# Routing logits of the attention stage in column groups of the array, turned back by one transpose

## What is computed

```python
x = x + 0.5 * ffn(layernorm(x), router_w, expert_bias, shared_w..., routed_w...)
x = x + attention(layernorm(x), W_q, W_k, W_v, W_o)
x = x + 0.5 * ffn(layernorm(x), router_w, expert_bias, shared_w..., routed_w...)
# in ffn:
scores = sigmoid(x @ router_w)                 # router_w is 256 x 16
_, top_idx = top_k(scores + expert_bias, 2)
```

## Time and profile before

| | us |
|---|---|
| median of 3 runs | 1482.68 |
| the three runs | 1480.43, 1482.68, 1484.01 |
| the profiled execution, its own time | 1479.03 |
| its span | 1477.0 |
| PE busy in the span | 1414.3 (96%) |
| granted TensorE clock, mean | 0.983 of full |

### The profile page before, as it was taken

How to read it: one execution, slowest core, us unless ns; L and a number is a source line. 1 busy time by engine, 2 the same in 40 slices (tenths; PEclk the granted TensorE clock), 3 DMA queues, 4 the chain that set the end, 5 groups by cost and what they waited for, 6 DMA issues and landing times. The chain is left out here.

```text
span 1477.0 us, 28613 instructions
## 1 busy us (share of the span) xinstructions
PE 1414.3 (96%) x8679; PEld 1154.1 (78%) x8712; DVE 956.1 (65%) x2269; ACT 660.6 (45%) x1347; POOL 585.7 (40%) x832
## 2 busy tenths in 40 slices
PE   5999999999989989999999999889999999999998
PEld 2688888888878876667767776568888888888887
DVE  5679865556555667777677766446776456565566
ACT  4534454343433444665666666544322343433332
POOL 6528820233333124464466444401388333333100
PEclk9999999999999998999999999889999999999999
DMA  9997998534396846454655555454464634356941
GB/s 343 332 340 266 329 368 343 183 111 140 104 329 213 300 123 155 96 137 129 148 128 135 142 136 127 156 189 172 150 243 150 231 105 147 104 209 206 306 134 53
DMA packets 175480, 284.75 MB, mean 193 GB/s; under 512 B 20708, under 2 KB 124644, under 8 KB 175092
## 3 DMA queue, kind: packets, MB, share of 16 engines
q1 hardware_dynamic: 133588, 205.26, 43.9%
q0 software_dynamic: 19104, 56.64, 10.6%
q10 hardware_dynamic: 22656, 21.11, 4.8%
HBM read 143.16 MB, written 109.84 MB: 171 GB/s over the span
## 5 line engine op out<-in xcount | busy, mean ns | idle before, releaser
L1717 PE MATMUL f_bank<-f_xparts,f_sw 128*128 128x512 f32 x1536 | 375.1, 394 | 3.4 <-DVEq L1647 3.3
L1717 PEld LDWEIGHTS f_bank<-f_xparts,f_sw 128*128 128x128 f32 x1536 | 282.6, 190 | 58.4 <-DVEq L1647 4.3
L1159 POOL DMA_INDIRECT outputs_by_choice<-f_yr,f_home x160 | 153.7, 960 | 355.4 <-DVE f_yr L1671 293.7
L2332 ACT ACTIVATE at_pT<-at_ps 128x512 f32<-128x512 f32 (+1 forms) x352 | 188.2, 560 | 64.5 <-PE at_ps L2598 58.0
L2260 POOL TENSOR_SCALAR_AFFINE_SELECT at_pT<-at_pT 128x128 f32<-128x128 f32 (+2 forms) x352 | 121.9, 354 | 199.9 <-ACT at_pT L2332 197.6
L1117 POOL DMA_INDIRECT rows_by_slot<-f_xq,slot x128 | 146.6, 1145 | 123.6 <-DVEq L1396 85.3
L1280 ACT CAST f_hparts<-f_hid 128x512 fp32r<-128x512 f32 x128 | 79.4, 620 | 206.8 <-DVE f_hid L1551 206.7
L1660 DVE TENSOR_TENSOR f_sil<-f_sil,f_bank 128x256 f32<-128x256 f32 x160 | 67.5, 422 | 159.9 <-ACT f_sil L1300 156.0
L1551 DVE TENSOR_TENSOR f_hid<-f_sil,f_bank 128x512 f32<-128x512 f32 x128 | 87.7, 685 | 117.7 <-PE f_bank L1717 106.7
L1731 PE MATMUL f_bank<-f_sw,f_hparts 128*128 128x256 f32 x1024 | 146.3, 286 | 2.0 <-ACT f_hparts L1280 1.7
L1731 PEld LDWEIGHTS f_bank<-f_sw,f_hparts 128*128 128x128 f32 x1024 | 137.4, 190 | 12.8 <-ACT f_hparts L1280 4.9
(11 more groups left out here) (268 smaller groups left out, 2665.3 us busy)
## 6 DMA issues: line engine op xcount, KB each, us to landing
f_ring<-weights_in_parts SPq DMA_DIRECT2D x32, 768.0 KB, 5.2
weights_in_parts<-fa_whi SPq DMA_DIRECT2D x30, 768.0 KB, 7.9
f_rawx<-rows_by_slot ACTq DMA_DIRECT2D x152, 128.0 KB, 2.1
at_whi<-weights_in_parts SPq DMA_DIRECT2D x16, 768.0 KB, 8.4
fa_ew<-in_L_ffn_routed_w_dram SPq DMA_DIRECT2D x42, 256.0 KB, 5.0
rows_by_slot<-zero POOLq DMA_DIRECT2D x10, 1024.0 KB, 22.5
f_xq<-xn_rows POOLq DMA_DIRECT2D x32, 256.0 KB, 4.0
fa_ew<-outputs_by_choice SPq DMA_DIRECT2D x8, 1024.0 KB, 8.6
```

Source lines behind the costliest of these rows:

```text
L1159: nc.gpsimd.indirect_dma_start(dram.yk, bass.IndirectOffsetOnAxis(ap=home[:, i:i + 1], axis=0), yr[:, i % 4, :], None).then_inc(y_st[i % 4 ...
L1717: ins = pe.matmul(ps[j % 2][:, :], sw12[:, wp, k, w, j * P:(j + 1) * P], xparts[:, u, xp, k, :], start=(i == 0), stop=(i == 3 * KD - 1))
L2332: s_.activation(pT[:, i % SLOTS, 0:w], ps2[i % RING2][:, 0:w], ACT.Exp).then_inc(ex_done, 1)
```

## The change

`route` now holds the router's 16 columns stationary and moves 128 columns of `xnT2` past them. The four row tiles t go to four column groups: the output of tile t, 16 logits x 128 rows, is on partitions 32t to 32t+15. This is again 8 matmuls. ACT copies the bank, 128 x 128, to a new tile `lT` (`logit_rows`). PE transposes `lT` in one instruction into the next `psX` bank (`spread`), and DVE copies the same 64 numbers per partition to `g.logits`, now out of four pieces 32 apart.

`route` moves from s = 9 to s = 8, directly behind `weigh`. `logit_rows` stands at s = 8 on ACT behind `copy_o`. `spread` and the DVE copy stand at s = 10. `AUX` has one entry more per chunk. The tile `lT` takes 512 bytes per partition of space that was free.

```diff
@@ attention_rows
+    r.lT = m.sb("lT", [P, P])
@@ attention: where the work stands
     def route_of(i, s):
-        return ours(i // NG - 2, 0, NB_) if i % NG == 1 and s == 9 else None
+        return ours(i // NG - 2, 0, NB_) if i % NG == 1 and s == AT_WEIGH else None
+
+    def spread_of(i, s):
+        return ours(i // NG - 2, 0, NB_) if i % NG == 1 and s == AT_WEIGH + 2 else None
@@ ACT, called behind copy_o
+            def logit_rows(c):
+
+                act.wait_ge(*full("route", c))
+                if c >= 1:
+                    act.wait_ge(*full("spread", c - 1))
+                sem, _ = gone("route", c)
+                s_.copy(lT[:], bank("route", c)[:, 0:P]).then_inc(sem, 1)
@@ DVE, called at s = 10 behind maxima
             def logits(c):
 
-                dve.wait_ge(*full("route", c))
-                sem, _ = gone("route", c)
-                v.tensor_copy(g.logits[:, bass.ds(c * (CT * E), CT * E)], bank("route", c)[:, 0:CT * E]
-                              ).then_inc(sem, 1)
+                dve.wait_ge(*full("spread", c))
+                sem, _ = gone("spread", c)
+                v.tensor_copy(g.logits[:, bass.ds(c * (CT * E), CT * E)].rearrange("p (t e) -> p t e", e=E),
+                              bank("spread", c)[:, 0:P].rearrange("p (t e) -> p t e", t=CT)[:, :, 0:E]).then_inc(sem, 1)
@@ PE, route called behind weigh, spread at s = 10 behind score2
-                for t in range(CT):
-                    for k in range(KD):
-                        ins = pe.matmul(bank("route", c)[:, t * E:(t + 1) * E], xnT2[:, k, t * P:(t + 1) * P],
-                                        g.rw[:, k, :], start=(k == 0), stop=(k == KD - 1))
+                for k in range(KD):
+                    for t in range(CT):
+                        ins = pe.matmul(bank("route", c)[32 * t:32 * t + E, 0:P], g.rw[:, k, :],
+                                        xnT2[:, k, t * P:(t + 1) * P], start=(k == 0), stop=(k == KD - 1),
+                                        skip_group_check=True)
                 ins.then_inc(sem, 1)
+
+            def spread(c):
+
+                sem = into("spread", c)
+                pe.wait_ge(*gone("route", c))
+                pe.transpose(bank("spread", c)[:, 0:P], lT[:], g.ident[:, :]).then_inc(sem, 1)
```

More of the change, by code:

```diff
@@ L497, in attention_rows @@
     r.mT = m.sb("mT", [P, 2, P], F32R)
+    r.lT = m.sb("lT", [P, P])
     r.pT = m.sb("pT", [P, len(UNITS1) + 4, CHUNK])
-    used = 4096 + 1024 + 2 * 128 + 512 + 1024 + 512 + 3 * 1024 + 80 + 5 * 1024 + 64 + 448 + 2 * 256 + 15 * CHUNK
+    used = 4096 + 1024 + 2 * 128 + 512 + 1024 + 512 + 3 * 1024 + 80 + 5 * 1024 + 64 + 448 + 2 * 256 + 128 + 15 * CHUNK
     m.sb("rest", [P, n - used])
@@ L2019, in attention @@
         for s in range(UN):
-            for kind, of in (("max", max_of), ("route", route_of), ("proj", proj_of), ("out", out_of),
-                             ("turn2", turn2_of), ("turn", turn_of), ("value", value_of)):
+            for kind, of in (("max", max_of), ("spread", spread_of), ("proj", proj_of), ("out", out_of),
+                             ("turn2", turn2_of), ("route", route_of), ("turn", turn_of), ("value", value_of)):
                 if of(i, s) is not None:
@@ L2035, in attention @@
         sums, turned, rec, attnT = mine.sums, mine.turned, mine.rec, mine.attnT
+        lT = mine.lT
         xres, xn2, xnT2, raw0 = mine.xres, mine.xn2, mine.xnT2, mine.raw0
@@ L2404, in _ @@
                         copy_o(i - 1)
+                    if route_of(i, s) is not None:
+                        logit_rows(route_of(i, s))
                     if turn_of(i, s) is not None:
@@ L2533, in _ @@
                         moments1(c + 2, s - 3)
-                    if route_of(i, s) is not None:
-                        logits(c - 2)
+                    if spread_of(i, s) is not None:
+                        logits(spread_of(i, s))
                     if s == AT_PROJ + 1 and proj_of(i, AT_PROJ) is not None:
@@ L2709, in _ @@
                         score2(u // UN, u % UN)
-                    if route_of(i, s) is not None:
-                        route(route_of(i, s))
+                    if spread_of(i, s) is not None:
+                        spread(spread_of(i, s))
                     if proj_of(i, s) is not None:
@@ L2719, in _ @@
                         weigh(i - 1)
+                    if route_of(i, s) is not None:
+                        route(route_of(i, s))
                     if turn_of(i, s) is not None:
```

## The result

| | before | after |
|---|---|---|
| median of 7 runs each, us | 1481.43 | 1472.86 |
| lowest and highest | 1478.37, 1484.01 | 1469.78, 1476.43 |
| the profiled execution | 1479.03 | 1471.12 |
| its span | 1477.0 | 1469.1 |

The ratio is 0.9945, with a 95% interval of 0.993 to 0.996: the change takes 8.6 us (0.55%) off. The forecast was 7.25 us less, 1475.4 us, with a range of 1472.0 to 1480.0. In a second comparison the same two kernels stood at 1475.56 and 1482.26 us, ratio 0.9948 (0.993 to 0.997), 6.7 us.

A forecast was written before the change was run, and what follows sets the result against it. PE was taken to bound the kernel, with DVE late just behind it at project_out. Six chunks' 6.0 us plus 1.25 us of clock, off the 1482.68 us median, gave 1475.4 us, range 1472 to 1480.

The forecast's parts named there:

- The bound: Attention stage: PE busy 226.91 of 230 us, so time leaving PE leaves the kernel unless another engine is late behind it.
- Removed, 1.71 us: PE, chunks 0 to 5: the old route's 16 records, 1.71 us from its start to the next score, go.
- The route, 0.46 us: PE behind weigh: the new route moves 512 columns at 0.89 ns each with four groups at once, 0.46 us a chunk.
- from above: Upper estimate for the new route on PE: groups in turn, 16 records of 0.114 us each, 1.83 us.
- The transpose, 0.1: PE, one added transpose per chunk: between zero and 0.15 us, taken as 0.1.
- DVE's chain: Maxima, logits copy and scale ahead of project_out: replayed, project_out starts 0.94 us earlier; gain taken as 1.0 a chunk, 6.0 for six.
- ACT's copy, nothing: ACT behind copy_o: the added 128 x 128 copy takes at most 0.39 us and costs nothing, with 0.45 us of cover.
- Chunk 6, nothing: Block's end: no gain or loss; the new chain ends near 973.0, 0.9 us inside the store's cover.
- The clock, 1.25 us: PE behind chunk 4's route: the clock's fall goes with the old route, 1.25 us back; other executions none or two.
- It comes back as a wait: Rival: late transposed logits or a longer DVE chain lose half of the 6.0 and the clock's part; 1479.7 us, chance 0.10.
- One group after another: Rival: column groups run in turn, +0.22 us on PE, DVE's chain later, +2.6 for six; 1485.3 us, chance 0.06.
- The loads are not hidden: Rival: each record also costs its load, route up to 3.6 us, some 2.2 us a chunk slower; 1496 us, chance 0.04.

The follow-up runs named there:

- after_four: Changed kernel with the 8 matmuls of each route issued four times; 64 records hold PE 1.86 us, ratio to the kernel before 0.9997.
- one_group: Changed kernel with all four row tiles in one column group, four transposes instead of one; route 1.84 us, ratio to the kernel before 0.9993.
- dve_three: Changed kernel with DVE copying the transposed logits three times; weigh's last record to the next round's 14.14 us, against 13.88 in the changed kernel.
- act_three: Changed kernel with ACT copying the route's bank three times; weigh's last record to the next round's 13.88 us, as in the changed kernel.
- tile_outer: Changed kernel with route's two loops exchanged, each row tile's matmuls together; route 0.57 us, ratio to the kernel before 0.9948.
- no_route: Changed kernel without the route, its copy, the transpose and the logits of chunks 0 to 6; median 1474.38 us against 1475.56, ratio to the kernel before 0.9941.
- after_again: Changed kernel, unchanged, for a second trace and comparison; median 1475.56 us, ratio to the kernel before 0.9948.

## Why the prediction was right

*The bound.* PE was the bound of the stage, and time taken from it left the kernel: the stretch, the round and the kernel fell together. But at project_out it was DVE, before and after, as the replay said. What no part of the prediction named are the DMAs of `at_rec` and `fa_qT` behind DVE; in chunk 0 they took 0.4 to 0.5 us of the gain in each of the two traces.

*Removed, 1.71 us:* as it was.

*The route, 0.46 us:* from weigh's last record to the score of s = 9 it was 0.20 us before and is 0.64 now, so 0.44. `after_four` gives the same 0.44, and `one_group` shows what it would be without the groups, 1.84 (1.83 given for "from above").

*The transpose, 0.1:* 0.03 us to its neighbour. It slips in under the scores around it; the lower bound was the right one.

*DVE's chain:* foreseen 0.94 us of gain, taken 1.0, measured 1.12 (project_out itself stands 1.10 us nearer to weigh). The steps were right and a little large: the copy costs 0.13 and not 0.2 (`dve_three`), and one maxima follows the other after 0.61 us and not 0.65. PE would have gained 1.71 - 0.44 - 0.03 = 1.24. So the term was mis-sized by 0.12 us a chunk: 6.7 us for six, not 6.0, less the 0.4 of chunk 0.

*ACT's copy, nothing:* right (`act_three`). It took 0.27 us, under the bound of 0.39.

*Chunk 6, nothing:* right. These are the lines that answer to the earlier trace rows; the last two are the copy of its logits on DVE and the next block's first matmul; the fence behind is the store's time to landing:

```profile
962.46 0.58 SPq L2235 DMA_DIRECT2D xn_turned<-at_xnT  x1
962.53 0.63 PE L2712 MATMUL at_psX<-at_xnT,rw 128*16 128x128 f32 x16 [1.61 <-ACT at_xnT L2387]
...
963.62 0.45 PE L2721 MATMUL at_psX<-ident,at_lT 128*128 128x128 f32 x1 [0.47 <-ACT at_lT L2395]
964.11 0.22 DVE L2514 COPY logits<-at_psX 128x64 f32<-128x64 f32 x1 [0.79 <-PE at_psX L2721]
...
966.55 0.77 PE L1718 MATMUL f_bank<-f_xparts,f_sw 128*128 128x512 f32 x1 [2.48 <-DVEq L1648]
```

```profile
xn_turned<-at_xnT SPq DMA_DIRECT2D x1, 512.0 KB, 3.1
```

The logits are there at 964.33, and the store, 3.1 us behind its issue, lands near 965.6. Before, the next block began 4.09 us behind the issue of the store (970.80 and 974.89), and now too (962.46 and 966.55).

*The clock, 1.25 us:* two traces of the kernel before show one fall behind a route each, at different chunks; with doubled routes there were three. In ten traces of kernels whose route moves 128 columns per load, 60 routes, there is none. That the fall came with the old route and went with it is supported by these counts, though the clock also fell where no route was near (926.0 in the kernel before). What of the route it was is not settled: the kind of matmul, its length and its place changed together, `after_four` and `one_group` match the length but stand behind weigh, and six routes each without a fall are weak evidence against one in six. The prediction stopped at chunk 4, and over the whole block the clock gave back nothing: in the two rounds behind chunk 5's it was 0.77 in both traces of the kernel before and 0.66 and 0.64 in those of the changed one, and they took 1.2 and 1.9 us longer. Of the other kernels made from the changed one, `tile_outer` has 0.77 and 22.03 us, the rest 0.64 to 0.71 and 22.83 to 23.85 us; `no_route`, with no route at all, is among them (0.70, 23.09 us). Whether the change lowers the clock there, or chance does, is open.

*The number, and luck.* The forecast was 7.25 us less, and the medians fell by 8.6 and 6.7 us. The six rounds, which are what the prediction was about, fell by 7.5 in both pairs. That the whole agrees with it is in part luck: 1.2 to 1.9 us were lost at the block's end, which the prediction did not foresee, and the time ahead of the first route and in the rounds without one varies by more than that.

*The rivals.* "It comes back as a wait" did not happen: project_out waited for DVE before and does now. Its wait grew from 0.11 to 0.24 us, which is the 0.12 us that DVE did not pass on; it was 0.69 in the one chunk of `after_again` where the DMA was late. "One group after another" is `one_group`, and the groups do work at once. "The loads are not hidden": 16 loads of 0.097 us, 1.55 us together, lie in a stream of 0.44 us. The 16 loads of `one_group`, as long, lie in 1.84 us of records that follow each other without a gap, so they overlap within one column group too. By the rule of the Trainium skill (TensorE: Matmul & The Clock Gate, The mechanism) a load overlaps matmuls in flight only in another row group; all groups here use all rows, and the loads overlap. The trace disagrees with that rule, and decides; a sentence of the same section that also lets a load run ahead into a background weight buffer it does not contradict.

## What to carry to other kernels

A small product in fp32 that holds the large operand stationary pays for the loads and not for the matmuls. Turning it round paid here only because the freed columns of the array were used by other tiles at once: the same small stationary operand in one group took 1.84 us, in four groups 0.55 (0.44 and a way out), against 1.71 before. Put such work next to other work in column groups, and read who is late just behind it before counting the gain: here DVE passed on 1.12 of 1.24 us, and moving one instruction on DVE gave another 0.46 in three of six rounds. In the other three a DMA came late there and took the gain back. So read not only who is late next, but who comes after that, and add up all rounds before calling a gain the kernel's.

## What the runs showed of the hardware that I had not expected

- Column groups worked at once whatever the order in which their matmuls were written. With each tile's matmuls together, the route took 0.57 us, and with the tiles in turn 0.55.
- A transpose of 128 x 128 in fp32 between scores moved its neighbour by 0.03 us, although the record is 0.27 us long.
- The TensorE clock fell to 1.2 GHz in the middle of work without a wait of PE just ahead, behind 16 or 32 records in a row with 16 moving columns each (2 of 12 and 3 of 6 routes); in the four cases with one fall in the stretch it cost 1.2 to 1.3 us.
- Executions of one kernel lay up to 17 us apart, while undisturbed intervals inside the block repeated mostly to 0.02 us. An effect of 0.1 us a chunk could be read from the trace, and from no number of timed runs made here.
